# An attention layer on one core: own rows filled and signalled apart, the embedding moved into batch 0

## The chip, the cores and the metric

The kernel runs on one core of a Trainium2 chip. The metric is the device time of one execution in microseconds. The kernel before has a median of 539.11 us over 3 runs (538.86 to 539.15).

The engines are TensorE (PE, matmuls and transposes), VectorE (DVE), ScalarE (ACT), GpSimd (POOL) and SyncE (SP, which here only issues transfers). Each works through its own instructions in order and waits on semaphores for the others.

## The reference

One conditioned attention block over 8 batches of 512 tokens, 256 features, 16 heads of 16.

```python
xn = layer_norm(x, norm_w, norm_b)
q = (xn @ q_w + q_b).reshape(Bx, Tx, H, -1)
k = (xn @ k_w + k_b).reshape(Bx, Tx, H, -1)
att = jnp.einsum('bnhl,bmhl->bnmh', q, k)
att = att + (1.0 - mask) * -1000000.0
att = jax.nn.softmax(att, axis=2)
v = ((xn @ v_w + v_b) * src_mask[:, :, None]).reshape(Bx, Tx, H, -1)
y = jnp.einsum('bnmh,bmhl->bnhl', att, v).reshape(Bx, Tx, Dx)
e = jax.nn.silu(emb) @ emb_w + emb_b
scale, shift = jnp.split(e[:, None, :], 2, axis=2)
h = layer_norm(y, sb_norm_w, sb_norm_b) * (1.0 + scale) + shift
h = jax.nn.silu(h) @ out_w + out_b
return x + h
```

The input `emb` is 8 x 512, so the embedding `e` (8 x 512) is computed once for all batches. It is first needed when batch 0's normed attention output is scaled and shifted.

## The kernel before, in words

A batch has 16 steps. A step is one chunk of 128 keys or queries (4 chunks) of one group of 4 heads (4 groups). In step t of batch b PE computes four score tiles (`st_unit`, L528), ACT takes their exponentials (L684), PE multiplies the previous step's exponentials with the values (`pv_step`, L547), and six steps ahead PE computes the scores a first time (`max_quad`, L496), only so that DVE can take each row's maximum (L862). Behind the scores of a step stands one further piece from a table (`JOBS`): a projection to q and k, to v, a transpose, the output projection. `body(b)` runs for b = -1 to 8. Body -1 is the opening, with jobs from `FIRST_JOBS`; from its step 10 on it runs the maximum matmuls of batch 0's steps 0 to 5. Bodies -1, 0 and 1 are written out, the next ones are a hardware loop, the last again written out.

The operands of the scores are rows in bf16: q and k are split into three parts (part 0, the rounded value; part 1, the rounded rest; part 2, the rest of that), so that products of parts add up to nearly f32. ACT or POOL makes part 0, DVE part 1, POOL part 2. `spread` on SP saves the parts of a head group (128 q and k columns) to memory in four copies: part 0 twice, part 1, part 2 (L1253), each counted by `copies_saved`. It then loads the mask rows (L1272) and, once all four saves are there, the rows `q_rows` and `k_rows` (`fill_rows`, L424). The rows lie in two halves of the partitions. Heads 0 and 1 of a group have their "own" rows (copies 0 to 2) in the first half and their rest rows (copies 1 to 3) in the second; heads 2 and 3 the other way round. A maximum matmul reads only a head's own rows, a score matmul both halves. Both wait for one semaphore per group, `rows_filled`, which counts ten transfers. In the opening ACT fills the second half of groups 0 and 1 from its own queue (`fill_half`).

The row maxima of a group are transposed by PE (`max_turn`, L506), split by DVE (L897, L899) and sent into `q_rows` (L1287, for the first group half of it from ACT, L747). The first score matmul waits for them.

The opening also loads all weights from SP: `weights_loaded` counts the q, k and v weights with their biases, and the first projection waits for all of them. The embedding's weights follow on SP's queue (L1242). The embedding itself (`embedding`, L466) runs in steps 11 to 14 of the opening, into the bank `pv_ps`; DVE reads and mixes it at the end of batch 0's step 0, and the first value matmul waits for `setup_done`.

`keep_warm` (L440) issues matmuls on zeros that nobody reads, to keep PE busy in waits of the opening: 5 behind step 2, 10 behind step 8, and 5 behind the maxima in each of steps 10 to 14.

Of the kernel before, what the change touches and what calls it, by code (L numbers as in the profile page):

```python
# [26 lines left out]
F32 = mybir.dt.float32  # L27
# [5 lines left out]
P = 128  # L33
# [7 lines left out]
KD = D // P  # L41
# [20 lines left out]
WEIGHT_DMAS = 2 * KD + 2 + 2  # L62
EMB_DMAS = 6
ROW_DMAS = 10
# [35 lines left out]
LATE_FIRST = {(8, 0): ("proj", 1, 1), (14, 1): ("proj", 2, 1)}  # L100
# [5 lines left out]
EMBEDDING_STEP = 11  # L106
WARM_FIRST = {2: 5, 8: 10}
WARM_MASK = 12
WARM_MAX = 5
# [75 lines left out]
def attention_layer(nc, x, cond, mask, norm_w, norm_b, q_w, q_b, k_w, k_b, v_w, v_b,  # L185
                    emb_w, emb_b, sb_w, sb_b, out_w, out_b, out):
    with ExitStack() as ctx:
# [91 lines left out]
        weights_loaded = sem("weights_loaded")  # L279
        mask_saved = sem("mask_saved")  # L280
        copies_saved = sem("copies_saved")
        rows_filled = [sem(f"rows_filled{i}") for i in range(NG)]
# [152 lines left out]
        def _(pe):  # L435
# [23 lines left out]
            def embedding(m):  # L459
# [4 lines left out]

                for k in range(KE):
                    mm = pe.matmul(pv_ps[:, m * B:(m + 1) * B], w_e[:, k, m * P:(m + 1) * P], cond_t[:, k, :],  # L466
                                   start=(k == 0), stop=(k == KE - 1))
                mm.then_inc(emb_ready, 1)

            def max_quad(b, t):  # L470
# [5 lines left out]
                if c == 0:  # L476

                    pe.wait_ge(rows_filled[g], ROW_DMAS * 16 * (mb + 1))
                    if isinstance(mb, int) and mb == 0 and g == 0:

                        pe.wait_ge(part0_ready, 2)
                        pe.wait_ge(v_plain_ready, 1)
                        pe.wait_ge(cond_ready, 1)
                for j in range(PAIRS):
# [9 lines left out]
                    for half in range(2):  # L494
# [3 lines left out]
                                  tile_position=(base, 0)).then_inc(max_ready, 1)  # L498

# [8 lines left out]
            def st_unit(b, t, h):  # L508
# [3 lines left out]
                if c == 0 and h == 0:  # L512

                    pe.wait_ge(max_filled[g], 2 * 16 * (b + 1))
# [16 lines left out]
            def pv_step(b, t):  # L531
# [39 lines left out]
            def job(t, b):  # L571
# [4 lines left out]
                if freed:  # L576

                    wait(pe, *freed)
                if kind == "proj":

                    if isinstance(d, int) and d == 0 and i == 0:
                        pe.wait_ge(weights_loaded, WEIGHT_DMAS * 16)
# [4 lines left out]

# [746 lines left out]
```

## Time and profile before

| | us |
|---|---|
| median of 3 runs | 539.11 |
| the profiled execution | 539.28 |
| its span in the profile | 537.6 |
| PE busy | 511.4 |
| DVE busy | 414.8 |
| ACT busy | 351.0 |
| POOL busy | 225.4 |

The span is the time between the first and the last instruction that the profile shows; some time lies around it. Busy time is summed over the span. A busy PE is not PE at its peak, since matmuls overlap. The granted clock is the share of 2.4 GHz that PE got in a stretch; 0.5 is 1.2 GHz.

### The profile page before, as it was taken

Reading aid. Unit: us, or ns where it says so; the run is one execution under the profiler, and the core shown is the slowest. Engines: PE = TensorE matmul, PEld = TensorE weight load, DVE = VectorE, ACT = ScalarE, POOL = GpSimd, SP = SyncE. Lnnn points to the kernel's source line nnn. Section 1 sums busy time; section 2 is a strip of 40 time slices with the busy share of each in tenths; the row PEclk is TensorE's granted clock in tenths of the full one; section 3 lists DMA queues with packets and bytes.
Section 4 is the critical chain, followed back from the end, with each engine's and each line's share of the span. In section 5 each row is a group of like instructions: output and inputs, shape, how many; then the busy total and the mean of one; then the engine's idle time right before and its main releaser. Section 6 shows DMA issues by size and latency. Waiting matters only on the chain.

```text
span 537.6 us, 10041 instructions
## 1 busy us (share of the span) xinstructions
PE 511.4 (95%) x2843; PEld 192.0 (36%) x2843; DVE 414.8 (77%) x661; ACT 351.0 (65%) x645; POOL 225.4 (42%) x270
## 2 busy tenths in 40 slices
PE   7798999899999999999999999999999999988987
PEld 3443333233334333433333333433333333422334
DVE  6587779877887878877887878878787877877625
ACT  2214777677776777677776777677776777566761
POOL 4535323536436443436336443536336443234011
PEclk9988999999999999999999999999999999999999
DMA  5643224343425334253425334253435332252021
GB/s 128 228 120 95 88 86 131 88 128 86 136 84 157 110 106 117 59 170 96 130 87 168 94 105 117 78 157 92 128 88 167 91 98 83 79 158 57 20 60 40
DMA packets 55050, 57.95 MB, mean 108 GB/s; under 512 B 12376, under 2 KB 42200, under 8 KB 55024
## 3 DMA queue, kind: packets, MB, share of 16 engines
q1 hardware_dynamic: 54480, 56.84, 35.8%
q10 hardware_dynamic: 544, 0.79, 0.5%
q8 instruction: 12, 0.20, 0.2%
q14 instruction: 14, 0.11, 0.1%
HBM read 36.35 MB, written 21.00 MB: 107 GB/s over the span
## 4 chain that ended last, share of the span: by engine, by line
PE 74%; ACT 9%; issue 8%; POOL 4%; DVE 2%; SPq 1%; DMA 1%; ACTq 0%; POOLq 0%; DVEq 0%
PE pv_ps L547 21%; PE st_ps L528 19%; PE mx_ps L496 11%; PE job_ps L585 7%; ACT probs L684 6%; PE job_ps L605 5%; PE job_ps L592 5%; PE mx_ps L630 3%; PE mx_ps L506 2%; ACT h_tanh L734 1%; DVE negmax L862 1%; PE mx_ps L635 1%; SPq L1233 1%; DMA vb_row<-in_L_cond_v_b 1%; POOL qk_parts L1135 0%
## 5 line engine op out<-in xcount | busy, mean ns | idle before, releaser
L862 DVE TENSOR_REDUCE negmax<-mx_ps 128x2 f32<-128x1024 f32 x256 | 303.4, 1220 | 86.9 <-PE mx_ps L496 85.9
L684 ACT ACTIVATE probs<-st_ps 128x512 f32<-128x512 f32 x502 | 273.3, 600 | 126.6 <-PE st_ps L528 126.0
L528 PE MATMUL st_ps<-q_rows,k_rows 115*128 115x512 bf16 x502 | 158.1, 385 | 6.1 <-ACT probs L684 3.4
L547 PE MATMUL pv_ps<-probs,v_rows 128*32 128x512 f32 x1024 | 136.4, 605 | 0.6 <-ACT probs L684 0.6
L496 PE MATMUL mx_ps<-k_rows,q_rows 51*128 51x512 bf16 x512 | 79.3, 383 | 6.4 <-DMA k_rows<-qk_dram 4.6
L1135 POOL TENSOR_TENSOR qk_parts<-qk_rest,qk_parts 128x512 bf16<-128x512 f32 x31 | 36.0, 1161 | 102.0 <-DVE qk_parts L936 102.0
L528 PEld LDWEIGHTS st_ps<-q_rows,k_rows 115*128 115x128 bf16 x502 | 38.7, 97 | 110.0 <-ACT probs L684 77.7
L1120 POOL TENSOR_TENSOR qk_parts<-qk_full,zero 128x512 bf16<-128x512 f32 x29 | 32.0, 1103 | 98.8 <-ACT qk_full L706 98.8
L585 PE MATMUL job_ps<-x_norm_t,w_qk 128*128 128x512 f32 x116 | 59.3, 604 | 0.0
L496 PEld LDWEIGHTS mx_ps<-k_rows,q_rows 51*128 51x128 bf16 x512 | 15.7, 94 | 112.4 <-issue 54.2
L1126 POOL TENSOR_TENSOR qk_rest<-qk_full,qk_parts 128x512 f32<-128x512 f32 x31 | 35.9, 1158 | 9.4 <-ACT qk_parts L698 7.1
L547 PEld LDWEIGHTS pv_ps<-probs,v_rows 128*32 128x32 f32 x1024 | 20.1, 108 | 33.1 <-issue 27.9
L592 PE MATMUL job_ps<-w_v,x_norm_t 128*128 128x256 f32 x120 | 30.7, 379 | 0.0
L605 PE MATMUL job_ps<-w_o,h_t 128*128 128x256 f32 x112 | 28.0, 381 | 0.0
L1193 POOL TENSOR_TENSOR x_res<-x_res,ob_row 128x1024 f32<-128x1024 f32 x8 | 18.9, 2358 | 21.6 <-DMA x_res<-in_x 21.6
L585 PEld LDWEIGHTS job_ps<-x_norm_t,w_qk 128*128 128x128 f32 x116 | 22.7, 196 | 11.8 <-issue 4.7
L706 ACT ACTIVATE qk_full<-job_ps,qkb_col 128x512 f32<-128x512 f32 x29 | 20.4, 704 | 8.6 <-PE job_ps L585 8.6
L592 PEld LDWEIGHTS job_ps<-w_v,x_norm_t 128*128 128x128 f32 x120 | 22.7, 190 | 6.2 <-issue 0.5
L1092 POOL TENSOR_TENSOR y_rstd<-y_vareps,exponent 128x4 f32<-128x4 f32 x7 | 7.1, 1019 | 40.9 <-DVE y_vareps L877 40.9
L1145 POOL TENSOR_TENSOR v_biased<-v_plain,vb_row 128x256 f32<-128x256 f32 x32 | 23.3, 727 | 1.1
L630 PE MATMUL mx_ps<-ident,y_t 128*128 128x128 f32 x128 | 19.8, 277 | 4.1 <-issue 2.1
L605 PEld LDWEIGHTS job_ps<-w_o,h_t 128*128 128x128 f32 x112 | 21.1, 190 | 6.4 <-issue 1.7
(116 smaller groups left out, 401.1 us busy)
## 6 DMA issues: line engine op xcount, KB each, us to landing
qk_dram<-qk_parts SPq DMA_DIRECT2D x128, 128.0 KB
q_rows<-qk_dram SPq DMA_DIRECT2D x124, 96.0 KB
k_rows<-qk_dram SPq DMA_DIRECT2D x124, 96.0 KB
x_in<-in_x SPq DMA_DIRECT2D x16, 256.0 KB, 3.0
x_res<-in_x SPq DMA_DIRECT2D x8, 512.0 KB, 3.9
out<-out_sb SPq DMA_DIRECT2D x16, 256.0 KB, 2.7
w_e<-in_L_cond_emb_w SPq DMA_DIRECT2D x1, 1024.0 KB, 5.7
k_rows<-mask_dram SPq DMA_DIRECT2D x64, 6.0 KB
```

Source lines behind the costliest of these rows:

```text
L496: pe.matmul(mx_ps[j][:, half, :], q_rows[base:base + ROWS_MX, g, h, c * P:(c + 1) * P], k_rows[base:base + ROWS_MX, g, h, :], start=True, ...
L528: pe.matmul(st_bank(b, t, h), k_rows[0:ROWS_ALL, g, h, c * P:(c + 1) * P], q_rows[0:ROWS_ALL, g, h, :], start=True, stop=True).then_inc(st ...
L547: mm = pe.matmul(pv_ps[VW * h:VW * (h + 1), :], v_rows[:, c, g * GH + h, :], probs[:, t % P_SLOTS, h, :], start=(c == 0), stop=(c == CH - ...
L585: mm = pe.matmul(ps, w_qk[:, k, i, :], x_norm_t[:, k, :], start=(k == 0), stop=(k == KD - 1))
L592: mm = pe.matmul(ps[:, c * D:(c + 1) * D], x_norm_t[:, k, tok:tok + P], w_v[:, k, :], start=(k == 0), stop=(k == KD - 1))
L605: mm = pe.matmul(ps[:, c * D:(c + 1) * D], h_t[:, k, tok:tok + P], w_o[:, k, :], start=(k == 0), stop=(k == KD - 1))
L630: mm = pe.transpose(ps[:, c * P:(c + 1) * P], y_t[:, c * P:(c + 1) * P], ident[:, :])
L684: act.activation(probs[:, t % P_SLOTS, h, :], st_bank(b, t, h), ACT.Exp).then_inc(exp_done, 1)
L862: dve.tensor_reduce(by_pair[:, :, j, c], mx_ps[j][:, :, :], AXIS_X, ALU.max, negate=True).then_inc(max_done, 1)
L1120: pool.tensor_tensor(qk_parts[:, 0, :], qk_full[:, :], zero[:, :].broadcast_to((P, T)), ALU.add).then_inc(part0_ready, 1)
L1126: pool.tensor_tensor(qk_rest[:, :], qk_full[:, :], qk_parts[:, 0, :], ALU.subtract).then_inc(rest_ready, 1)
L1135: pool.tensor_tensor(qk_parts[:, 2, :], qk_rest[:, :], qk_parts[:, 1, :], ALU.subtract).then_inc(part2_ready, 1)
```

## The change

Five things are done.

1. Own rows are filled first. `rows_filled` becomes `own_filled` (six transfers: two of mask rows, four of own rows) and `rest_filled` (four). The part 2 save counts on `rest_saved`, the other three on `copies_saved`. Own fills wait for three saves, rest fills for the fourth. The maximum matmuls wait for `own_filled`, the scores for `rest_filled` too.
2. The embedding's matmuls move from the opening to batch 0's steps 13 to 15 (one, two and one of its four column blocks), into `job_ps`. DVE reads them at the start of batch 1 and mixes them at the end of its step 0.
3. The nine loads for it (w_e now in four) go out on ACT's queue, one each in batch 0's steps 0, 1, 2, 3, 5, 6, 7, 9 and 10, before the third exponential.
4. The warm-up matmuls are laid otherwise: 4 in place of 10 behind step 8, and 3 behind each pair of maximum matmuls up to batch 0's step 6 (6 behind the last of the first group).
5. In the opening, the first maximum pair no longer waits for the second group's part 0 (only the second pair does), the k and v weights are signalled apart, the second memset of `k_rows` moves ahead of the first group's parts, that of `v_rows` behind the second group's third part, and DVE casts the second group's part 1 behind the first two reductions.

```diff
-WEIGHT_DMAS = 2 * KD + 2 + 2
-EMB_DMAS = 6
-ROW_DMAS = 10
+QK_DMAS = 2 * KD + 2
+V_DMAS = 2
+EMB_DMAS = 9
+OWN_DMAS = 6
+REST_DMAS = 4
...
-LATE_FIRST = {(8, 0): ("proj", 1, 1), (14, 1): ("proj", 2, 1)}
+LATE_FIRST = {(11, 0): ("proj", 1, 1), (14, 1): ("proj", 2, 1)}
...
-EMBEDDING_STEP = 11
-WARM_FIRST = {2: 5, 8: 10}
+EMBEDDING = {13: (0,), 14: (1, 2), 15: (3,)}
+EMBEDDING_LOADS = (0, 1, 2, 3, 5, 6, 7, 9, 10)
+WARM_FIRST = {2: 5, 8: 4}
 WARM_MASK = 12
-WARM_MAX = 5
+WARM_MAX = {(0, 0): 3, (0, 1): 3, (1, 0): 3, (1, 1): 3, (2, 0): 3, (2, 1): 3, (3, 0): 3, (3, 1): 6,
+            (4, 0): 3, (4, 1): 3, (5, 0): 3, (6, 0): 3}
...
-        def fill_rows(engine, i, half):
+        def fill_rows(engine, i, half, own):
 
             at = HALF * half + PARTS
-            for own in range(2):
-                heads = slice(PAIRS * own, PAIRS * (own + 1))
-                for side, rows in enumerate((q_rows, k_rows)):
-                    engine.dma_start(rows[at:at + ROWS_PROD, i, heads, :].rearrange("p h t -> p (h t)"),
-                                     copies(i, side, own, half != own)).then_inc(rows_filled[i], 16)
+            heads = slice(PAIRS * own, PAIRS * (own + 1))
+            filled = own_filled[i] if half == own else rest_filled[i]
+            for side, rows in enumerate((q_rows, k_rows)):
+                engine.dma_start(rows[at:at + ROWS_PROD, i, heads, :].rearrange("p h t -> p (h t)"),
+                                 copies(i, side, own, half != own)).then_inc(filled, 16)
+
+        def fill_halves(engine, i, halves, n):
+
+            engine.wait_ge(copies_saved, 16 * PARTS * (n + 1))
+            for half in halves:
+                fill_rows(engine, i, half, half)
+            engine.wait_ge(rest_saved, 16 * (n + 1))
+            for half in halves:
+                fill_rows(engine, i, half, 1 - half)
...
-                    pe.wait_ge(rows_filled[g], ROW_DMAS * 16 * (mb + 1))
-                    if isinstance(mb, int) and mb == 0 and g == 0:
-
-                        pe.wait_ge(part0_ready, 2)
-                        pe.wait_ge(v_plain_ready, 1)
-                        pe.wait_ge(cond_ready, 1)
+                    pe.wait_ge(own_filled[g], OWN_DMAS * 16 * (mb + 1))
+                first = isinstance(mb, int) and mb == 0
                 for j in range(PAIRS):
+                    if first and step == 0:
+
+                        if j == 0:
+                            pe.wait_ge(xt_ready, KD)
+                            pe.wait_ge(cond_ready, 1)
+                        else:
+                            pe.wait_ge(v_plain_ready, 1)
+                        pe.wait_ge(part0_ready, j + 1)
...
+                    if first:
+
+                        keep_warm(pv_ps, WARM_MAX.get((step, j), 0))
...
+                    pe.wait_ge(rest_filled[g], REST_DMAS * 16 * (b + 1))
                     pe.wait_ge(max_filled[g], 2 * 16 * (b + 1))
...
-                    if isinstance(b, int) and b == 0 and g == 0:
-
-                        pe.wait_ge(setup_done, 1)
                     pe.wait_ge(v_ready, NG * b + g + 1)
...
+                if isinstance(b, int) and b == 1 and t == 0:
+
+                    pe.wait_ge(setup_chain, 6 + 2 * KD)
...
-                    if isinstance(b, int) and b == -1 and 0 <= t - EMBEDDING_STEP < 2 * KD:
-                        embedding(t - EMBEDDING_STEP)
+                    if isinstance(b, int) and b == 0 and t in EMBEDDING:
+                        for m in EMBEDDING[t]:
+                            embedding(m)
...
+                    if isinstance(b, int) and b == 0 and t in EMBEDDING_LOADS:
+                        load_embedding(EMBEDDING_LOADS.index(t))
                     exp_unit(b, t, 2)
                     exp_unit(b, t, 3)
```

On PE, before, the opening from the turn of the condition to the transpose of the first group's maxima (`mx_ps0`, `mx_ps1` are the banks of the two maximum pairs, `warm_in` marks a warm-up matmul, `w_e` the embedding; the rows left out repeat these):

```order
L456 MATMUL st_ps1<-ident,cond_silu 128x8 x4
L440 MATMUL pv_ps<-warm_in 128x512 x10
L496 MATMUL mx_ps0<-k_rows,q_rows 128x512 x2
L496 MATMUL mx_ps1<-k_rows,q_rows 128x512 x2
L440 MATMUL st_ps1<-warm_in 128x512 x5
...
L466 MATMUL pv_ps<-cond_t,w_e 128x8 x4
...
L506 MATMUL mx_ps1<-ident,negmax 16x128
```

And in the changed kernel:

```order
L474 MATMUL st_ps1<-ident,cond_silu 128x8 x4
L458 MATMUL pv_ps<-warm_in 128x512 x4
L519 MATMUL mx_ps0<-k_rows,q_rows 128x512 x2
L458 MATMUL pv_ps<-warm_in 128x512 x3
L519 MATMUL mx_ps1<-k_rows,q_rows 128x512 x2
...
L458 MATMUL pv_ps<-warm_in 128x512 x6
L532 MATMUL mx_ps1<-ident,negmax 16x128
```

The warm-up matmuls moved from behind two pairs to behind each pair, and the embedding is gone from here.

On PE, in the changed kernel, the end of batch 0 from the transposes of step 13 on (before, these rows stand without those that name `w_e`):

```order
L659 MATMUL mx_ps0<-ident,y_t 128x128 x4
L485 MATMUL job_ps<-cond_t,w_e 128x8 x4
L555 MATMUL st_ps0<-q_rows,k_rows 128x512
L555 MATMUL st_ps1<-q_rows,k_rows 128x512
L532 MATMUL mx_ps1<-ident,negmax 16x128
...
L485 MATMUL job_ps<-cond_t,w_e 128x8 x8
L555 MATMUL st_ps0<-q_rows,k_rows 128x512
```

Each part of the embedding stands straight before the next step's first two score matmuls.

On SP's queue, before, the first group's rows, with what each waits for:

```order
L1253 DMA qk_dram<-qk_parts 8x16x512 [waits part2_ready]
L1272 DMA k_rows<-mask_dram 3x2x512 [waits k_preset,q_preset,mask_saved]
L1272 DMA k_rows<-mask_dram 3x2x512
L424 DMA q_rows<-qk_dram 48x1x1024 [waits copies_saved]
L424 DMA k_rows<-qk_dram 48x1x1024
L424 DMA q_rows<-qk_dram 48x1x1024
```

And in the changed kernel:

```order
L1295 DMA qk_dram<-qk_parts 8x16x512 [waits part2_ready]
L1314 DMA k_rows<-mask_dram 3x2x512 [waits k_preset,q_preset,mask_saved]
L1314 DMA k_rows<-mask_dram 3x2x512
L433 DMA q_rows<-qk_dram 48x1x1024 [waits copies_saved]
L433 DMA k_rows<-qk_dram 48x1x1024
L433 DMA q_rows<-qk_dram 48x1x1024 [waits rest_saved]
```

The order of the four fills is the same; the first two now wait for three saves and the next two for the fourth. For groups 2 and 3, and in all later batches, SP fills four own rows and then four rest rows, where before own and rest alternated.

## Rows read from the trace of the kernel before

**Rows 1.** The page: share of the span per engine, then the granted clock (tenths).

```profile
PE 511.4 (95%) x2843; PEld 192.0 (36%) x2843; DVE 414.8 (77%) x661; ACT 351.0 (65%) x645; POOL 225.4 (42%) x270
...
PEclk9988999999999999999999999999999999999999
```

**Rows 2.** The chain of waits, whole span: start us, us, what.

```profile
103.68 0.99 PE pv_ps L547 x8
...
164.33 0.99 PE pv_ps L547 x8
...
224.99 1.00 PE pv_ps L547 x8
```

**Rows 3.** Timeline of PE: start us, us, what, count, idle time before and its releaser.

```profile
20.62 2.33 PE L440 MATMUL pv_ps<-warm_in 128*128 128x512 bf16 x10
27.58 0.60 PE L496 MATMUL mx_ps<-k_rows,q_rows 51*128 51x512 bf16 x4 [4.62 <-DMA k_rows<-qk_dram]
28.11 2.28 PE L440 MATMUL st_ps<-warm_in 128*128 128x512 bf16 x5
...
42.67 0.60 PE L528 MATMUL st_ps<-q_rows,k_rows 115*128 115x512 bf16 x2
...
45.35 1.04 PE L528 MATMUL st_ps<-q_rows,k_rows 115*128 115x512 bf16 x2
46.17 3.12 PE L585 MATMUL job_ps<-x_norm_t,w_qk 128*128 128x512 f32 x4
...
49.66 1.06 PE L547 MATMUL pv_ps<-probs,v_rows 128*32 128x512 f32 x8
```

**Rows 4.** Timeline of SP's queue, opening: start us, us, what.

```profile
10.93 0.43 SPq L1242 DMA_DIRECT2D w_e<-in_L_cond_emb_w  x1
...
14.79 2.57 SPq L1253 DMA_DIRECT2D qk_dram<-qk_parts  x4
...
22.11 0.64 SPq L424 DMA_DIRECT2D q_rows<-qk_dram  x1
```

**Rows 5.** Timeline of SP's queue, batch 0: the same for a later group.

```profile
71.19 1.86 SPq L1253 DMA_DIRECT2D qk_dram<-qk_parts  x2
...
75.11 0.61 SPq L424 DMA_DIRECT2D q_rows<-qk_dram  x1
```

**Rows 6.** Timeline of ACT and its queue, opening and batch 0.

```profile
22.86 0.80 ACTq L424 DMA_DIRECT2D k_rows<-qk_dram  x1
...
24.33 0.61 ACTq L424 DMA_DIRECT2D k_rows<-qk_dram  x1
...
51.62 1.08 ACT L684 ACTIVATE probs<-st_ps 128x512 f32<-128x512 f32 x2 [0.62 <-PE st_ps L528]
```

**Rows 7.** Timeline of DVE, opening.

```profile
28.03 2.36 DVE L862 TENSOR_REDUCE negmax<-mx_ps 128x2 f32<-128x1024 f32 x2 [0.65 <-PE mx_ps L496]
...
36.37 2.36 DVE L862 TENSOR_REDUCE negmax<-mx_ps 128x2 f32<-128x1024 f32 x2 [0.16 <-PE mx_ps L496]
...
39.41 0.28 DVE L899 TENSOR_TENSOR max_parts<-mx_ps,max_parts 16x128 bf16<-16x128 f32 x1
...
42.59 4.62 DVE L862 TENSOR_REDUCE negmax<-mx_ps 128x2 f32<-128x1024 f32 x4 [0.31 <-PE mx_ps L496]
```

**Rows 8.** Stretches of the opening: busy us of each engine, granted clock, DMA.

```profile
28.00:32.00 4.00, 4.00 (x14) 1.09 (x13) 3.35 (x3) 0.00 (x0) 3.25 (x5) 0.57 0.36 102
45.00:48.00 3.00, 2.99 (x7) 1.35 (x8) 2.96 (x8) 1.08 (x2) 2.03 (x4) 0.54 0.24 76
```

**Rows 9.** Timeline of PE, the end of batch 0 and its handover.

```profile
95.47 0.63 PE L630 MATMUL mx_ps<-ident,y_t 128*128 128x128 f32 x4 [0.64 <-issue]
...
99.38 0.88 PE L528 MATMUL st_ps<-q_rows,k_rows 115*128 115x512 bf16 x2 [0.47 <-ACT probs L684]
...
105.58 1.88 PE L585 MATMUL job_ps<-x_norm_t,w_qk 128*128 128x512 f32 x4
```

**Rows 10.** Timeline of PE, opening: one quarter of the embedding.

```profile
32.52 0.95 PE L466 MATMUL pv_ps<-cond_t,w_e 128*128 128x8 f32 x8
```

More of the change, by code:

```diff
@@ L278, in attention_layer @@
         norm_loaded = sem("norm_loaded")
-        weights_loaded = sem("weights_loaded")
+        qk_loaded = sem("qk_loaded")
+        v_loaded = sem("v_loaded")
         mask_saved = sem("mask_saved")
         copies_saved = sem("copies_saved")
-        rows_filled = [sem(f"rows_filled{i}") for i in range(NG)]
+        rest_saved = sem("rest_saved")
+        own_filled = [sem(f"own_filled{i}") for i in range(NG)]
+        rest_filled = [sem(f"rest_filled{i}") for i in range(NG)]
         max_filled = [sem(f"max_filled{i}") for i in range(NG)]
@@ L586, in job @@
                 elif kind == "vproj":
+                    if isinstance(d, int) and d == 0:
+                        pe.wait_ge(v_loaded, V_DMAS * 16)
                     pe.wait_ge(xt_ready, KD * (d + 1))
@@ L747, in place_first_max, with load_embedding @@
                 act.dma_start(max_row(0, 1), max_parts[:, 0, 1:2, :]).then_inc(max_filled[0], 16)
+            def load_embedding(n):
+                with nc.allow_non_contiguous_dma(reason="small vectors, once"):
+                    loads = [(w_e[:, k, :], emb_w[k * P:(k + 1) * P, :]) for k in range(KE)]
+                    loads += [(sbw_col[:, :], sb_w.rearrange("(k p) -> p k", p=P)),
+                              (sbb_col[:, :], sb_b.rearrange("(k p) -> p k", p=P)),
+                              (eb_col[:, :], emb_b.rearrange("(k p) -> p k", p=P)),
+                              (ob_row[:, :], out_b.rearrange("(a n) -> a n", a=1).broadcast_to((P, D))),
+                              (w_o[:, :, :], out_w.rearrange("(k p) n -> p k n", p=P))]
+                    assert len(loads) == len(EMBEDDING_LOADS) == EMB_DMAS
+                    dst, src = loads[n]
+                    act.dma_start(dst, src).then_inc(emb_loaded, 16)
             def yt_copy(b, t):
@@ L1043, in body @@
                     stats_at(b, t, 2)
-                    if t == 0 and isinstance(b, int) and b == 0:
-                        embedding()
+                    if t == 0 and isinstance(b, int) and b == 1:
+                        mix_embedding()
                     if t == TURN_STEP - 1 and isinstance(b, int) and b == -1:
@@ L1198, in body @@
                 take_part2(b, 1, 1)
+                if isinstance(b, int) and b == -1:
+                    preset_v()
                 if exists(b + 1):
@@ L1273, in spread @@
                                      mask_dram[bass.ds(d, 1)].rearrange("a s t -> (a s) t").unsqueeze(1).broadcast_to(
-                                         (PARTS, PAIRS, T))).then_inc(rows_filled[i], 16)
+                                         (PARTS, PAIRS, T))).then_inc(own_filled[i], 16)
                 if exists(d):
-                    sp.wait_ge(copies_saved, 16 * COPIES * (n + 1))
-                    for half in range(1 if first and i < 2 else 2):
-                        fill_rows(sp, i, half)
+                    fill_halves(sp, i, range(1 if first and i < 2 else 2), n)
             def place_max(b, i):
```

47 lines of the change are left out of this document (20 added, 27 removed).

## The prediction

> **What bounds the kernel now.** I read the page first. TensorE (PE) is busy 95% of the span, and its clock is at full nearly everywhere but in the second to fourth of the 40 slices [rows 1]. A weight matmul's busy time can hide waits, so I then read the chain of waits: the attention-value matmuls in step 0 of batch 1 start at 103.68 us, those in step 0 of batch 2 at 164.33, of batch 3 at 224.99 [rows 2]. A batch costs 60.65 us when written out and 60.66 us in the loop. Neither the amount of PE work in a full batch nor its order is touched by the change, so I keep the later batches at this price. What is left is the opening, before the first value matmul at 49.66 [rows 3], and batch 0, where the embedding is put.
>
> In the timeline of the opening PE sits idle 4.62 us, until 27.58, for row fills [rows 3]. What follows is paced by VectorE (DVE): a pair of its maximum reductions takes 2.36 us, four back to back take 4.62, so 1.155 each [rows 7]. The first starts at 28.03, the eighth ends at 36.37 + 2.36 = 38.73, and only then can the first group's maxima be split (39.41 + 0.28 = 39.69) and sent to the row memory. The first score matmuls run at 42.67, the second pair at 45.35 [rows 3]. The clock is at 0.57 of full in 28 to 32 and at 0.54 in 45 to 48 us [rows 8], both after PE had been idle or thinly used. These are spells at 1.2 GHz.
>
> **Term 1, the first own rows.** The maximum matmuls read only own heads' rows. Today they wait for all eight fills, and these for all four saves. SP issues the saves from 14.79 to 17.36, and its first fill starts at 22.11 [rows 4], 4.75 us after the last issue ended. For a later group the last issue ends at 71.19 + 1.86 = 73.05 and the fill starts at 75.11, 2.06 us after [rows 5]. The opening differs in what stands before it on SP's queue: w_e, 1 MB, issued at 10.93 [rows 4], and w_o behind it. Both are gone in the changed order.
>
> I take 2.06 us. The third save's issue ends at about 14.79 + 3/4 x 2.57 = 16.72, so its data are there at 18.78, when SP has also finished the fourth save and the mask rows. SP and ScalarE (ACT) each issue two own fills of 0.61 us [rows 6], until 20.0. Today the last fill is issued until 24.33 + 0.61 = 24.94 [rows 6] and the matmul starts 2.64 us later; half as many bytes are in flight after the change, so I put 2.4 there. The matmuls then start at 22.4 in place of 27.58: 5.2 us less. The lower bound is 2.06 us for the fill too, 22.1. The upper one keeps the 4.75 for the saves: 16.72 + 4.75 + 1.22 + 2.64 = 25.3, a gain of 2.2. The second pair also waits for ACT's cast of the second projection, which stands behind ACT's four fills: 18.8 + 4 x 0.61 = 21.2, and a cast of under a microsecond, so it is done by 22 and hidden.
>
> The Trainium skill, page "DMA: Bandwidth & Descriptors", section "Queues, rings and completion order", says that SP's transfers lie on one row of rings and each engine takes them in the order of the ring. By that rule the saves really stood behind w_e, and term 1 is 5.2. The same page of the Trainium skill, section "Issuing engines are not separate DMA queues", says that another issuing engine brings no bandwidth, only issue time; by that, putting w_e on ACT's queue alone would bring nothing, and the gain is that it goes out after 40 us. The rows agree with an early backlog, and don't tell order from contention.
>
> **Term 2, the pace of the reductions.** Today 11.15 us pass from the first maximum matmul to the end of the eighth reduction, with warm-up and embedding matmuls between steps. In the changed order three warm-up matmuls stand behind each pair: at full clock 3 x 0.23 (ten take 2.33 [rows 3]) and a pair's 0.3, some 1.0 us, under the 1.155 of the reduction that runs meanwhile. So 0.45 + 8 x 1.155 + 0.43 for the cast of the second group, which moves from before the reductions to behind the first two: 10.1. That is 1.0 less. The 0.31 us of idle time before 42.59 [rows 7], behind an embedding quarter, goes too: 0.3. From the split on, 39.69 to 45.35, the same four reductions and cast remain, and I keep the length.
>
> The moved cast delays the second group's saves: it comes at 22.4 + 0.45 + 2.3 = 25.2, while its rows are first read after the eighth reduction, at 32.5. Save 0.6, landing 2.06, two fills 1.2 and 2.6 make 31.7; thus hidden with 0.8 us to spare. POOL's memset of the value rows now runs after that group's third part, and the values are read only by the value matmuls, at about 42. The first pair of maxima is sent at 33.5 and lands before PE has finished the sixth step's matmuls at 36.7, as now.
>
> **Term 3, the clock.** The projection at 46.17 takes 3.12 us at 1.2 GHz [rows 3]; the same four matmuls take 1.88 at 105.58 [rows 9]. PE now has a warm-up triple in step (6,0) and idles about 1 us instead of 4.62 before the maxima. I take full clock there: 1.2 less. The bound on the other side is nothing gained.
>
> **Term 4, the embedding in batch 0.** A quarter takes 0.95 us of PE [rows 10], four 3.8. In batch 0 the steps 13 to 15 have no output projection. In step 13 the quarter stands behind the transposes that end at 96.1, straight before the next scores, whose exponentials are long done; the 0.64 us gap lies before the transposes [rows 9], so it isn't filled: 0.95 added. In step 14 two quarters, 1.9, meet a wait of 0.47 and a second one of about 0.3 inside the 0.88 us pair [rows 9]: 1.1 added. In step 15 one quarter meets the like: 0.1. Together 2.1; bounds 1.0 and 3.8. DVE's reading of the result stands at the head of batch 1, where DVE waits for PE anyway, and PE's new wait for it stands before the projection at 105.58, two pairs of scores and the value matmuls later; the mixing stands behind the next reductions. I take nothing for them.
>
> **Term 5, nine loads on ACT's queue.** One issue costs 0.61, at worst 0.80 [rows 6]. Each stands before the third exponential, where ACT waits for scores; the shortest of the nine waits is 0.62 [rows 6]. I take 0.2 in all; bounds 0 and 1.6. Behind a late issue stand two exponentials, and PE's next scores wait for them. The data are needed in step 13, three steps after the last load, so no landing is waited for.
>
> In the loop PE has one more wait per group (rest rows, filled before the old wait would have ended) and POOL one register step; batches 1 and 2 above show that register waits cost nothing: 0.
>
> **Sum.** -5.2 - 1.0 - 0.3 - 1.2 + 2.1 + 0.2 = -5.4. The profiled execution took 539.28 us (span 537.6), 0.17 above the median of 539.11, so 539.28 - 5.4 = 533.9.
>
> **Rivals.** A, the saves land no sooner: contention or the write itself set 4.75 us, not w_e. For it: a load issued at 10.93 should be over well before 22. Then the start is 25.3, PE has idled 3.8 us, and the clock falls as it did at 28; two places at 1.2 GHz lose 0.65 each. -2.2 - 1.0 - 0.3 + 1.3 - 1.2 + 2.3 = -1.1: 538.2. Against it is the 2.06 of every later group.
>
> B, the moved work isn't hidden: the embedding costs its 3.8 and ACT 1.6, 3.1 more than I took: 537.0. For it speaks that batch 0's steps are held by the chain score, exponential, score.
>
> C, the other side: the warm-up itself becomes the bound. At 1.2 GHz five warm-ups take 2.28 us [rows 3], so three 1.3, and a pair of maxima 0.5: 1.8 against 1.155, 0.65 lost in each of the 12 places where a group of warm-ups now stands behind a pair. If the clock stays down through the opening, +7.8, and the 1.2 of term 3 is lost: 542.9. It is slower than before from about the seventh such place on (4.2 / 0.65). Against it: the clock came back by 32 us in [rows 8] once PE was full.
>
> D, more is hidden: start at 22.1, embedding 1.0, ACT nothing: -6.9, 532.4; with the same earliness for the second group and the 0.15 us that the first projection gains by no longer waiting for the value bias, 532.
>
> **Chances.** My forecast 0.66, A 0.12, B 0.09, C 0.04, D 0.09. Its own range is 532.5 to 535.5; for 8 in 10 it reaches to D's end and most of B: 531.6 to 537.0. About 0.2% (1.1 us) is what a measurement tells from no change: A lies on that edge, half of it counts as same. Faster 0.89, same 0.06, slower 0.05.
>
> **What would show it.** The first maximum matmul near 22.4 (25 would be A); reductions 1.155 apart; the second pair of scores near 38.9 and a projection of 1.9 us behind it; the first value matmul 7.7 us earlier than 49.66; the opening value matmul of batch 1 only 5.4 earlier than 103.68, and batches still 60.66 apart. It is wrong if the clock's row shows a spell at half after 25 us, if ACT's third exponentials start late by more than 0.2 us, or if the later batches change their price.

## The result and the profile after

The changed kernel takes 534.07 us (median of 4 runs, 533.08 to 534.89) against 539.13 (538.86 to 539.34) for the kernel before: ratio 0.9898, 95% interval 0.9885 to 0.9911. It is faster by 1.0%, and the forecast was 533.9. The profiled execution took 533.38 us with a span of 531.7. In a later group one execution of the kernel before took 1080.95 us; it is left out of every median and ratio.

The page of the changed kernel, busy time of PE and the granted clock, as [rows 1]:

```profile
PE 510.8 (96%) x2851; PEld 190.9 (36%) x2851; DVE 414.4 (78%) x661; ACT 351.0 (66%) x645; POOL 225.4 (42%) x270
...
PEclk9999999999999999999999999999999999999999
```

PE does the same work. The 8s in the third and fourth slices are gone. The chain of waits, value matmuls in step 0 of batches 1 to 3, as [rows 2]:

```profile
97.77 0.99 PE pv_ps L571 x8
...
158.42 0.99 PE pv_ps L571 x8
...
219.08 0.99 PE pv_ps L571 x8
```

Batches are still 60.65 and 60.66 us apart. From 97.77 to the end of the span are 433.9 us, and from 103.68 to the end before it were 433.9 too. So all 5.9 us of this pair of executions lie ahead of batch 1. The opening in the timeline of PE, as [rows 3]:

```profile
20.52 1.04 PE L458 MATMUL pv_ps<-warm_in 128*128 128x512 bf16 x4
23.43 0.39 PE L519 MATMUL mx_ps<-k_rows,q_rows 51*128 51x512 bf16 x2 [1.88 <-DMA k_rows<-qk_dram]
23.75 0.82 PE L458 MATMUL pv_ps<-warm_in 128*128 128x512 bf16 x3
...
33.42 0.28 PE L532 MATMUL mx_ps<-ident,negmax 128*16 128x128 f32 x1 [0.47 <-DVE negmax L906]
33.63 0.39 PE L519 MATMUL mx_ps<-k_rows,q_rows 51*128 51x512 bf16 x2
...
37.74 0.59 PE L555 MATMUL st_ps<-q_rows,k_rows 115*128 115x512 bf16 x2 [0.37 <-DMA q_rows<-max_parts]
...
39.66 0.60 PE L555 MATMUL st_ps<-q_rows,k_rows 115*128 115x512 bf16 x2
40.11 1.88 PE L612 MATMUL job_ps<-x_norm_t,w_qk 128*128 128x512 f32 x4
...
42.35 1.06 PE L571 MATMUL pv_ps<-probs,v_rows 128*32 128x512 f32 x8
```

The first maximum matmul starts 4.15 us earlier than before, the first scores 4.93, the first value matmul 7.31. SP's queue, as [rows 4], and under it ACT's:

```profile
14.69 2.57 SPq L1295 DMA_DIRECT2D qk_dram<-qk_parts  x4
...
19.15 0.64 SPq L433 DMA_DIRECT2D q_rows<-qk_dram  x1
```

```profile
19.23 0.64 ACTq L433 DMA_DIRECT2D q_rows<-qk_dram  x1
19.91 0.80 ACTq L433 DMA_DIRECT2D k_rows<-qk_dram  x1
...
38.16 0.60 ACT L711 ACTIVATE probs<-st_ps 128x512 f32<-128x512 f32 x1 [5.71 <-PE st_ps L555]
38.38 0.41 ACTq L786 DMA_DIRECT2D w_e<-in_L_cond_emb_w  x1
38.65 0.59 ACT L711 ACTIVATE probs<-st_ps 128x512 f32<-128x512 f32 x1
```

The first fill goes out 2.96 us earlier than [rows 4] had it, and two fills fewer stand ahead of the first matmul on each queue. The issue of w_e runs while the exponential ahead of it still works. DVE, as [rows 7], and the stretches of [rows 8]:

```profile
23.89 2.36 DVE L906 TENSOR_REDUCE negmax<-mx_ps 128x2 f32<-128x1024 f32 x2 [3.08 <-PE mx_ps L519]
26.16 0.42 DVE L980 CAST qk_parts<-qk_rest 128x512 bf16<-128x512 f32 x1
26.49 6.87 DVE L906 TENSOR_REDUCE negmax<-mx_ps 128x2 f32<-128x1024 f32 x6
```

```profile
28.00:32.00 4.00, 4.00 (x20) 1.21 (x19) 4.00 (x4) 0.24 (x1) 3.64 (x5) 1.00 0.50 148
...
45.00:48.00 3.00, 2.53 (x16) 0.55 (x17) 2.10 (x6) 2.04 (x4) 1.49 (x3) 1.00 0.62 186
```

Six reductions stand back to back, and the clock is 1.00 where it was 0.57 and 0.54. The price of the embedding is read in the chain of waits of the changed kernel, steps 13 to 15 of batch 0, as [rows 9]:

```profile
85.45 1.00 PE pv_ps L571 x8
...
87.52 0.64 issue
88.16 0.63 PE mx_ps L659 x4
88.79 0.79 PE job_ps L485 x8
...
90.14 0.99 PE pv_ps L571 x8
...
92.21 1.69 PE job_ps L485 x16
...
94.35 0.99 PE pv_ps L571 x8
```

The same steps in the kernel before:

```profile
92.76 0.99 PE pv_ps L547 x8
...
96.83 0.99 PE pv_ps L547 x8
...
100.25 1.00 PE pv_ps L547 x8
```

The first two steps take 4.69 and 4.21 us; before they took 4.07 and 3.42. The third takes 3.42 (94.35 to 97.77), as before. That is 1.41 us in all.

### The profile page after: what moved, and what is told of

Read it like the earlier page. It is cut to its first block, busy times and chain, and to the rows that moved or that the text cites. A ratio compares the mean times of both kernels' runs of the same rounds, so it can differ in the third digit from the quotient of the medians.

```text
span 531.7 us, 10099 instructions
## 1 busy us (share of the span) xinstructions
PE 510.8 (96%) x2851; PEld 190.9 (36%) x2851; DVE 414.4 (78%) x661; ACT 351.0 (66%) x645; POOL 225.4 (42%) x270
## 4 chain that ended last, share of the span: by engine, by line
PE 76%; ACT 9%; issue 6%; DVE 4%; POOL 3%; DMA 1%; ACTq 0%; SPq 0%; POOLq 0%; DVEq 0%
PE pv_ps L571 21%; PE st_ps L555 19%; PE mx_ps L519 11%; PE job_ps L612 7%; ACT probs L711 6%; PE job_ps L634 5%; PE job_ps L621 5%; PE mx_ps L659 3%; DVE negmax L906 2%; PE mx_ps L532 2%; ACT h_tanh L761 1%; PE mx_ps L664 1%; DMA k_rows<-qk_dram 1%; PE job_ps L485 1%; DMA x_in<-in_x 1%
## 5 line engine op out<-in xcount | busy, mean ns | idle before, releaser
L612 PE MATMUL job_ps<-x_norm_t,w_qk 128*128 128x512 f32 x116 | 58.0, 592 | 0.0
```

What stands on the lines that cost most here:

```text
L612: mm = pe.matmul(ps, w_qk[:, k, i, :], x_norm_t[:, k, :], start=(k == 0), stop=(k == KD - 1))
```

## The experiments

Each was timed with the kernel before on the same chip. Three groups: the first with before at 539.85 us (538.65 to 540.86), the second at 539.45 (539.07 to 541.84), the third at 540.27 (538.85 to 540.87). "The changed kernel" means the one of the same group where it ran. In the second group it did not run; there the ratios to the kernel before are compared. A ratio is one of means, so where executions scatter it can differ from the ratio of the medians.

### The changed kernel again

> The changed kernel again, as the base that the other three are compared with on the same chip. Its four times so far lie in two pairs, 533.1 to 533.4 and 534.8 to 534.9. Theory: the profile shows the first maximum matmul at about 23.4 us, the second pair of scores at 39.7 and batches of 60.66; if the slower pair has a cause in the opening, the profile of a slower execution shows the first maximum matmul some 1.5 us later. Rival: the 1.5 us come from elsewhere in the span.

Measured 534.24 us (532.9 to 534.61, 4 runs), ratio 0.9899 (0.9873 to 0.9925). Its profiled execution took 534.21 and starts late: the first projection by 1.48 us (12.88 against 11.40), the first maxima by 0.88 (24.31 against 23.43), the first value matmul by 0.79 (43.14 against 42.35). ACT's first fill is 1.54 us late (20.77 against 19.23); the rest is scatter in the landing, since the rows were there 2.08 us after the last issue of the own fills, and not 2.72. So the slower kind loses its 1.5 us ahead of the fills, as the theory had it, and here got 0.6 of it back by a faster landing.

### Own and rest rows split in the kernel before, nothing else

```diff
-ROW_DMAS = 10
+OWN_DMAS = 6
+REST_DMAS = 4
...
-                    pe.wait_ge(rows_filled[g], ROW_DMAS * 16 * (mb + 1))
+                    pe.wait_ge(own_filled[g], OWN_DMAS * 16 * (mb + 1))
```

> The kernel before with only the split of the rows (own fills first, after three saves; two semaphores); embedding, loads, warm-up and casts stay. Theory (w_e's load ahead of the saves on SP's queue is most of the delay): the third save lands at about 21.4, the first maximum matmul starts at about 25.7 instead of 27.6, the clock still falls to half; gain 1.7 to 2, so about 537.3. Rival (the split carries the gain): the first maximum matmul at 23.4 and a time near 535.

Measured 536.87 us (535.73 to 541.12, 10 runs), ratio 0.9964 (0.9939 to 0.9989). By the medians the split alone is worth 3.0 of the 5.6 us; by the ratio, 1.9, since two of the ten executions took 541.1. PE in this kernel, whose first projection started 1.3 us late in the profiled execution (the start-up, below):

```profile
21.88 2.33 PE L452 MATMUL pv_ps<-warm_in 128*128 128x512 bf16 x10
24.69 0.61 PE L508 MATMUL mx_ps<-k_rows,q_rows 51*128 51x512 bf16 x4 [0.48 <-DMA k_rows<-qk_dram]
...
46.20 1.07 PE L560 MATMUL pv_ps<-probs,v_rows 128*32 128x512 f32 x8 [0.59 <-DVE mod_half L861]
```

The saves were issued from 16.05 on and the first fill at 21.01, 3.0 us after the third save's issue ended. The expectation had the clock fall to half, and in this execution it did not: after 0.48 us of idle time the projection at 43.30 takes 1.88. The other executions differ in this. Those with a mean granted clock of 0.996 or more took 535.7 to 536.7 us, the three with 0.993 or 0.994 took 537.1 to 538.0, the two with 0.986 took 541.1. The 0.59 us of the last line is a new wait: once the rows come earlier, the first value matmul waits for the mixing of the embedding, which the change moves away.

### The embedding's loads back on SP's queue in the opening

```diff
-                    if isinstance(b, int) and b == 0 and t in EMBEDDING_LOADS:
-                        load_embedding(EMBEDDING_LOADS.index(t))
...
+                loads = [(sbw_col[:, :], sb_w.rearrange("(k p) -> p k", p=P)),
...
+                         (w_e[:, :, :], emb_w.rearrange("(k p) n -> p k n", p=P)),
+                         (w_o[:, :, :], out_w.rearrange("(k p) n -> p k n", p=P))]
```

> The changed kernel with the embedding's loads (w_e in one piece) back on SP's queue before the second x load, everything else as changed. Theory: the saves again land behind w_e, first own fill at about 21.4, first maximum matmul at 25.5 to 26 instead of 23.4, PE idles 4 us, clock at half for a while: 2.3 + 1 us more than the changed kernel, about 537. Rival: saves land as in the changed kernel (first fill at 19.2), time 534.

Measured 536.26 us (535.66 to 537.82, 4 runs), ratio 0.9938 (0.9916 to 0.9961): 2.0 above the changed kernel. SP's queue, and under it PE:

```profile
10.92 0.43 SPq L1278 DMA_DIRECT2D w_e<-in_L_cond_emb_w  x1
...
14.51 2.74 SPq L1289 DMA_DIRECT2D qk_dram<-qk_parts  x4
...
21.26 0.64 SPq L433 DMA_DIRECT2D q_rows<-qk_dram  x1
```

```profile
25.71 0.61 PE L519 MATMUL mx_ps<-k_rows,q_rows 51*128 51x512 bf16 x2 [4.34 <-DMA k_rows<-qk_dram]
27.65 0.61 PE L519 MATMUL mx_ps<-k_rows,q_rows 51*128 51x512 bf16 x2
```

With w_e and w_o ahead, the saves are reported 4.7 us after the third one's issue ended (14.51 + 3/4 x 2.74 = 16.57, and 21.26), without them 2.5 (14.69 + 3/4 x 2.57 = 16.62, and 19.15). In the kernel above, whose saves went out 1.5 us later behind the same loads, the fill started at 21.01: a set time, not a set delay. The DMA engines show the backlog: in 13 to 15, 15 to 17 and 17 to 19 us they are busy for 1.00, 0.98 and 0.87 of the time, in the changed kernel for 0.02, 0.24 and 0.52. The loads themselves are over sooner: w_e is there 5.9 us after its issue, w_o 6.3 us after, and the x load behind them up to 6.7, which is about 19.2. That excludes rival A, by which the saves land no sooner without the loads. Whether the saves wait in order or share the engines was not told apart, and the six loads moved together, so the share of w_e alone isn't known either.

The second row shows rival C at work in small: after 4.34 us of idle time two pairs of maxima are 1.94 us apart and not 1.08. The clock came back after three such pairs, with the warm-ups still running. This execution took 537.82 us, the slowest of the four, with a mean granted clock of 0.994; the other three have 0.997 and 535.66 to 536.37. Its first value matmul is at 46.77, 4.4 us behind that of the changed kernel's first profiled execution: 2.3 of it is the later rows (25.71 against 23.43), the rest the spell. The 2.0 us of the medians hold less of the spell.

### Batch 0's rows filled together, after all four saves

```diff
+            if isinstance(n, int) and n < NG:
+                engine.wait_ge(rest_saved, 16 * (n + 1))
+                for half in halves:
+                    for own in range(2):
+                        fill_rows(engine, i, half, own)
+                return
...
                     pe.wait_ge(own_filled[g], OWN_DMAS * 16 * (mb + 1))
+                    if isinstance(mb, int) and mb == 0:
+                        pe.wait_ge(rest_filled[g], REST_DMAS * 16)
```

> The changed kernel with batch 0's rows filled in the old order after all four saves, and its maximum matmuls waiting for all ten transfers; later batches as changed. Theory: first fill at 19.8, eight fills in flight, first maximum matmul at about 25.0 instead of 23.4, and the second group's rows are late as well, so some 1.5 to 2.5 us more: 535.5 to 536.5. Rival: the split brings nothing once w_e is gone, since the eight fills land together anyway: 534.

Measured 539.95 us (539.05 to 541.57, 10 runs), ratio 1.0011 (0.9997 to 1.0026): nothing of the gain is left, 3.5 us more than the expectation allowed. The first maxima start 1.8 us later than in the changed kernel, and a second wait shows up at the second group. The expectation had left out the clock: the first wait, 3.76 us, is followed by a spell at 1.2 GHz, in which the first pairs are 1.78 and 1.92 us apart and not 1.08. PE of this kernel:

```profile
25.23 0.45 PE L527 MATMUL mx_ps<-k_rows,q_rows 51*128 51x512 bf16 x2 [3.76 <-DMA k_rows<-qk_dram]
...
38.60 0.39 PE L527 MATMUL mx_ps<-k_rows,q_rows 51*128 51x512 bf16 x2 [2.00 <-DMA k_rows<-qk_dram]
40.19 0.61 PE L527 MATMUL mx_ps<-k_rows,q_rows 51*128 51x512 bf16 x2
```

VectorE's cast makes the second group's part 1, POOL makes part 2 from it, and the cast stands behind the first two reductions. Here the group's saves are issued until 31.07 and its fills from 33.15, because every row waits for part 2 too. In the changed kernel the saves are issued until 28.41, and the own fills go out at 29.28 without waiting for the fourth to land. SP still issues that save and the mask rows first (until 29.23); ACT's own fills go out at 29.22, so this order cost nothing, but it had nothing to spare. After the 2.00 us of idle time the clock is low again: the next two distances between pairs are 1.59 and 1.94 us, not 1.08.

### The same, with the second group's cast back before the reductions

```diff
-LATE_FIRST = {(11, 0): ("proj", 1, 1), (14, 1): ("proj", 2, 1)}
+LATE_FIRST = {(8, 0): ("proj", 1, 1), (14, 1): ("proj", 2, 1)}
```

> The kernel in which batch 0's rows are filled together after all four saves (539.95 us), but with VectorE's cast for the second group back before the reductions. Theory (the late cast needs the split: the second group's rows came 2.0 us late there, and TensorE fell to 1.2 GHz in that wait): the wait at the fifth step goes and the projection at the end of the opening takes 1.9 us; first maximum matmul at 25.2 as there, median 536.5 to 538.0. Rival (the rows of group two are late by the longer fills, whatever the cast): the wait of about 2 us stays, 539.5 to 540.2.

Measured 537.79 us (536.54 to 538.63, 7 runs), ratio 0.9957 (0.9942 to 0.9973). The wait at the second group is gone (PE goes from the transpose at 36.26 to the maxima at 36.47) and the first maxima stay at 25.27. So the loss is two things: the first rows, 3.2 us against the changed kernel of its group (534.56), and the moved cast, about 2.5 us (the rest of 5.7; by the two ratios, 1.0011 and 0.9957, 2.9). The 3.2 are more than the delay of the rows. In the profiled execution the first maxima come 1.8 us later than in the changed kernel (25.27 against 23.43), the wait of 3.78 us ahead of them is followed by a spell at 1.2 GHz that costs another 1.0 (the eighth reduction ends at 36.20 against 33.36), and the third group's rows are late by 0.47 us at 50.71. The split takes from the moved cast what it costs here.

### The changed kernel with only the cast back

The edit of the experiment above, on the changed kernel.

> The changed kernel with DVE's cast of the second group's part 1 back ahead of the first reduction. Theory: DVE then waits for POOL's rest, ready at about 24.0, and starts the first reduction at 24.5 instead of 23.9, but the cast no longer stands between reductions (0.43), so the eighth ends at most 0.3 later and the second group's rows come 1.8 us earlier: within 0.3 us of the changed kernel. Rival: the second group's rows are what the fifth step waits for in the changed kernel, and the time falls by up to 1 us.

Measured 533.4 us (533.14 to 534.71, 4 runs), ratio 0.9886 (0.9852 to 0.992). The first value matmul of batch 1 is at 97.75, against 97.77, so with the split it matters little where the 0.42 us cast stands. The two traces are not quite alike, though: here the rows were there 0.52 us earlier (first maxima at 22.91), and the eighth reduction still ended 0.08 later (33.44), because VectorE waited for POOL until 23.95 and then cast. So the later place may be worth up to half a microsecond in an execution in which the rows come early.

### No warm-up matmuls between the maxima

```diff
-WARM_MAX = {(0, 0): 3, (0, 1): 3, (1, 0): 3, (1, 1): 3, (2, 0): 3, (2, 1): 3, (3, 0): 3, (3, 1): 6,
-            (4, 0): 3, (4, 1): 3, (5, 0): 3, (6, 0): 3}
+WARM_MAX = {}
```

> The changed kernel without the warm-up matmuls between the maximum matmuls (37 fewer; the others stay). Theory: the reductions still run 1.155 us apart, since they and not PE set the pace, but PE is thinly used from 23.4 on and its clock falls to half; the projection behind the second pair of scores takes 3.1 instead of 1.9 us: 1.2 to 2.5 us more, 535.3 to 536.6. Rival (the warm-ups cost as much as they give): same or faster than the changed kernel.

Measured 535.46 us (534.88 to 536.8, 4 runs), ratio 0.9914 (0.9882 to 0.9946). PE of this kernel, and one stretch (columns as in [rows 8]):

```profile
24.89 0.60 PE L518 MATMUL mx_ps<-k_rows,q_rows 51*128 51x512 bf16 x4 [1.43 <-DMA k_rows<-qk_dram]
...
42.26 3.10 PE L611 MATMUL job_ps<-x_norm_t,w_qk 128*128 128x512 f32 x4
```

```profile
34.00:38.00 4.00, 2.14 (x7) 0.43 (x7) 3.49 (x6) 0.00 (x0) 1.93 (x3) 0.50 0.49 157
```

PE is busy for only half of the stretch and at 1.2 GHz, and the projection behind it takes 3.10 in place of 1.88. That is the 1.2 us of term 3. The reductions keep their pace without the warm-ups: from the first maxima to the end of the eighth reduction are 9.95 us, against 9.93. From the first maxima to the first value matmul are 20.84 us against 18.92, so in the trace the warm-ups are worth 1.9. The ratios (0.9914 and 0.9899) give 0.8 us, with intervals that overlap, and the profiled execution (536.8) was the slowest of the four and started late. But all four have a mean granted clock of 0.984, where the changed kernel has 0.997 to 1.000 in all its executions. So the lower clock is shown; what it costs lies between 0.8 and 1.9 us.

### Three quarters of the embedding left out

```diff
-                for k in range(KE):
+                for k in range(1):
...
-                                   start=(k == 0), stop=(k == KE - 1))
+                                   start=True, stop=True)
```

> The changed kernel with three quarters of the embedding's matmuls left out (only the first of four blocks of its sum is computed), so PE has 0.25 instead of 0.95 us per column block. The traces of before and after show 1.4 us added in batch 0's steps 13 to 15. Theory: with a quarter of the work steps 13 and 14 lose at most 0.2 each, and the kernel is 1.0 to 1.4 us faster, about 532.8. Rival (the waits and not the matmuls cost): the same time.

Measured 532.9 us (532.47 to 533.4, 4 runs), ratio 0.9867 (0.9837 to 0.9898). Steps 13 to 15 take 4.08, 3.42 and 3.42, as before the change. Its profiled execution (533.4) has its first value matmul at 43.73, as a late one of the changed kernel has (43.71, 534.76 us, in the third group), and takes 1.36 us less. So the embedding in batch 0 costs the 1.4 us that the chain shows, and nothing elsewhere.

### Step 13's block ahead of the transposes

```diff
                     job(t, b)
+                    early = isinstance(b, int) and b == 0 and t == 13
+                    if early:
+                        embedding(0)
                     side(t, b)
...
-                        for m in EMBEDDING[t]:
+                        for m in EMBEDDING[t][1 if early else 0:]:
```

> The changed kernel with step 13's column block of the embedding ahead of the transposes of that step instead of behind them. Theory: PE waits 0.64 us there for the reduction, so the block fills this gap, and of the 0.62 us that step 13 lost some 0.3 to 0.6 come back: about 0.5 us faster. Rival (the transposes come later and with them DVE and the next transposes of the maxima): the same.

Measured 533.99 us (532.64 to 534.39, 4 runs), ratio 0.9893 (0.9862 to 0.9924). PE in step 13:

```profile
87.17 0.96 PE L485 MATMUL job_ps<-cond_t,w_e 128*128 128x8 f32 x8
87.98 0.63 PE L659 MATMUL mx_ps<-ident,y_t 128*128 128x128 f32 x4
```

The 0.64 us gap before the transposes is filled, and the step takes 4.07 again. The 0.6 us stands in the trace and is not seen in four runs that scatter by 1.7. So the scatter was next.

### The start-up: three kernels with five rounds

In five of the fourteen profiled executions the first projection starts 1.3 to 1.9 us late; in a sixth, that of the last kernel of this section, the warm-up matmuls run as slowly but are fewer. In the timeline of PE the two executions of the changed kernel are told apart by these rows, first the one of the result, then the one run again:

```profile
6.15 2.76 PE L458 MATMUL pv_ps<-warm_in 128*128 128x512 bf16 x12
...
11.40 1.96 PE L612 MATMUL mx_ps<-x_norm_t,w_qk 128*128 128x512 f32 x4 [0.18 <-ACT x_norm_t L738]
```

```profile
5.84 4.91 PE L458 MATMUL pv_ps<-warm_in 128*128 128x512 bf16 x12
...
12.88 1.96 PE L612 MATMUL mx_ps<-x_norm_t,w_qk 128*128 128x512 f32 x4 [0.18 <-ACT x_norm_t L738]
```

Twelve warm-up matmuls, 0.23 us each, take 0.41 each in the second, and the transposes of the input queue behind them although VectorE has it ready at 8.8. The edit is `WARM_MASK = 12` to `WARM_MASK = 7`, alone and together with the block of step 13; the changed kernel ran beside them.

> The changed kernel once more, as the partner of the three that run with it. The executions seen so far stand at 533.1 to 533.4 or at 534.2 to 534.9. Theory (start-up): in some executions the twelve warm-up matmuls behind the mask's transposes take 4.9 us in place of 2.8, and the first projection starts 1.5 us later; so both kinds should show again, about 533.2 and 534.5, median 533.2 to 534.6. Rival (scatter from elsewhere): where the twelve take 2.8 us the time can be 534.5 too.

> The changed kernel with seven warm-up matmuls in place of twelve behind the mask's transposes, nothing else. Theory (start-up): the slower kind of execution goes; all near 533.2, median 533.0 to 533.5, highest under 534. Rival (the clock falls in the idle time): 535 or more. Rival (scatter from elsewhere): executions at 534.5 stay as frequent as they are.

> The changed kernel with seven warm-up matmuls in place of twelve behind the mask's transposes, and with step 13's block of the embedding ahead of the transposes. At 0.41 us each seven take 2.9 us, from 5.8 to 8.7, before the normed input is there at 9.0, so that a slow start costs nothing. Theory (start-up): every execution is at the fast kind's time less the 0.6 us of step 13: 532.4 to 532.9, median about 532.6, ratio to the changed kernel 0.997. Rival (the clock falls in the 1.5 us of idle time that a fast start now leaves before the input's transposes): the first projections take 3.1 in place of 1.9 us each, and the median is 535 or more.

| | median us | range | ratio to before |
|---|---|---|---|
| changed kernel | 534.56 (6 runs) | 532.97 to 536.11 | 0.9898 (0.9878 to 0.9918) |
| seven warm-ups | 533.91 (4) | 533.9 to 534.1 | 0.9887 (0.9869 to 0.9906) |
| seven, and step 13's block moved | 532.71 (4) | 532.41 to 533.57 | 0.9867 (0.9848 to 0.9887) |

The changed kernel showed both kinds again, as expected. With seven warm-ups the scatter shrank, but "seven warm-ups" alone missed its 533.0 to 533.5 by 0.4, and its highest (534.1) the limit of 534. Its trace shows a part of the reason:

```profile
24.38 1.31 PE L458 MATMUL pv_ps<-warm_in 128*128 128x512 bf16 x3
25.62 0.60 PE L519 MATMUL mx_ps<-k_rows,q_rows 51*128 51x512 bf16 x2
26.16 1.46 PE L458 MATMUL pv_ps<-warm_in 128*128 128x512 bf16 x3
```

Here PE idled 1.61 us before the maxima, less than the 1.88 of the changed kernel, and yet fell to 1.2 GHz for about 3 us, which put the first value matmul at 42.85 in place of 42.35 although the first maxima came 0.45 us earlier. It isn't the whole reason: two of the four executions have a mean granted clock of 1.000, where this one has 0.997, and took 533.92 and 533.90 all the same. What decides whether such a spell comes is open. The last kernel has the lowest median of all that compute the whole result: its four executions all lie below the median of the changed kernel beside it. The two intervals overlap slightly, so its gain of 1.7 us (by the ratios) is likely, not proven. Its profiled execution had a slow start (seven warm-ups in 3.17 us), and the first projection still began at 11.76, within 0.6 us of the fast starts (11.22 to 11.40). That the start-up makes the scatter is thus likely and not shown: the times of single executions fit it, but one kernel (the split alone) started late and was the second fastest of its ten.

## Why the prediction was right

The sum came out at 533.9 and the median at 534.07. The mechanisms of its four large terms were found; the sizes were off by up to 1 us, both ways. Term by term, in the profiled execution:

**Term 1, first own rows: -5.2 predicted, -4.15 measured.** This is the term that was mis-sized most. The mechanism held: the saves landed early without the loads ahead of them, as the early-loads kernel shows. The missing 1.03 us are in three places. The saves took 2.5 us and not 2.06, so that ACT's first fill went out at 19.23 (0.45 later than 18.78). Two issues on ACT took 1.48 and not 1.22 (0.26); the 0.80 of the second stood in [rows 6], and I had taken 0.61 for both. From the end of the last issue to the matmul were 2.72 us (20.71 to 23.43) and not 2.4 (0.32). The first two hardly change in later runs of the changed order: with the loads moved away, SP's first fill starts 4.26 to 4.53 us after its first save in nine executions. The third is scatter: with four fills ahead it is 2.08 to 2.91 us in eleven executions, with a median of 2.50, so 2.4 was a fair value and this execution drew a long one.

**Term 2, pace: -1.0 and -0.3 predicted, -1.22 and -0.33 measured.** From the first maxima to the end of the eighth reduction are 9.93 us (23.43 to 33.36) against 11.15; from the split's end at 34.33 to the second score pair 5.33 against 5.66. That the warm-ups stay under the reductions is shown (1.08 us between pairs); which of the moved pieces sets the new pace was not taken apart, only that it isn't the warm-ups. The second group's rows were the weak point. I gave them 0.8 us to spare, with the last fill issued at 29.06. In fact their own fills were issued until 30.72: the first maxima and reductions were 0.96 later, the cast's own 0.42 was missing from my sum, and the two issues took 1.44 and not 1.2. With the 2.1 to 2.9 above they land between 32.8 and 33.6, with their first matmul at 33.63: between 0.8 us and nothing. The joint-filling kernel shows what it costs if they are late. The first group's maxima did not land before PE was free, as I had put it: the first scores waited 0.37 us for them, at no cost, since VectorE's reductions went on back to back.

**Term 3, clock: -1.2 predicted, -1.24 measured** (3.12 to 1.88), and 3.10 again without the warm-ups. The low clock lies in the third and fourth of the 40 slices, not in the second to fourth as I read it; nothing in the sum hangs on that. I had left out that the score pair ahead of the projection ran at 1.2 GHz too: from 45.35 to the projection at 46.17 were 0.82 us, now 0.45 (39.66 to 40.11), another 0.37.

The opening's terms together: -7.7 predicted. Measured -4.15 - 1.22 - 0.33 - 1.24 - 0.37 = -7.31, which is what the first value matmul shows.

**Term 4, embedding: +2.1 predicted, +1.41 measured.** Step 13 cost 0.62 and not 0.95, step 14 0.79 and not 1.1, step 15 nothing. A block stands in the chain with 0.79 us, not with the 0.95 that the opening's row showed as its busy time; consecutive groups overlap. I had taken the busy time of one group as its length in a chain. Rival B's 3.8 is excluded by the chain and by the quarter-embedding kernel.

**Term 5, loads on ACT: +0.2 predicted, 0 measured.** From the value matmuls of step 2 to those of step 13 (46.50 to 85.45) are 38.95 us, the same as before (53.81 to 92.76), and from those of step 1 to those of step 2 are 4.08 us in both (42.35 to 46.43, 49.66 to 53.74). An issue takes 0.34 to 0.41 us here and runs beside the exponential ahead of it.

Altogether -7.31 + 1.41 = -5.90 at the opening value matmul of batch 1, against -5.4; the profiled execution took 533.38. The median is 0.7 us above it, and that execution had a fast start. The close hit of the median is thus partly luck: the terms were off by +1.05 (1), -0.25 (2), -0.41 (3), -0.7 (4) and -0.2 (5), and the scatter between executions, probably of the start-up, which I had not looked for, stands on the other side.

Taken out of the changed kernel, the loads' new place is worth 2.0 us and the split 3.2, or 5.7 where the cast stays late. Put into the kernel before, the split alone is worth 3.0 by the medians and 1.9 by the ratio. So what a part is worth hangs on the others: the late cast costs 2.5 us without the split and about nothing with it, and with the split alone a wait of 0.59 us for the embedding comes up. Moving the embedding out of the opening was not tested by itself.

## What to carry to other kernels

When an early consumer reads only part of a buffer, give that part its own semaphore and save and fill it first; then a late producer of the other part matters only through what the queue still issues ahead of the fills. Bulk loads that nobody needs soon belong behind the first latency-bound round trip, not ahead of it on the queue. Where warm-up matmuls stand in the program order ahead of real work, count them at half clock (0.39 to 0.41 us each in five of the fourteen executions, and not 0.23), and read a chain for the length of a group, not its busy time.

## What the runs showed of the hardware

- The same twelve warm-up matmuls at the start ran in 2.76 or in 4.91 us from one execution to the next, while the granted clock is 1.00 in that stretch in both. The column does not show this start-up; the mean time of a matmul does.
- The third save, of 128 x 512 in bf16, was reported 2.5 us after its issue ended where the queue had been free for 2 us ahead of the group's saves, and 4.7 us after where w_e and w_o stood ahead. Saves issued 1.5 us apart behind the same loads were reported at nearly the same time (21.01 and 21.26 us).
- From the last issue of the fills to the waiting matmul are 2.08 to 2.91 us with four fills ahead of it and 2.64 to 2.65 with eight (three executions). Half the bytes bring little, if anything.
- PE fell to 1.2 GHz after 1.61 us of idle time in one kernel and not after 1.88 in another, which differs only by five warm-up matmuls some 15 us earlier; nor after 1.95 in the kernel with step 13's block moved.
- The same kernel can have more or fewer such spells from one execution to the next: the split alone ran with a mean granted clock of 1.000 at 535.73 us and of 0.986 at 541.12.
